# A quantized feed-forward block on one core: twelve conv spans evicted by ScalarE and GpSimd, and a reordered start

## What is computed

```python
# x (128, 32, 512); conv weight (32, 8, 9), four groups of channels
y   = conv1d(x, weight, pad=4, groups=4) + (cond @ c_weight.T + bias)[:, :, None]
gate = qlinear(y, w_gate)       # w_gate, w_up (1376, 512)
up   = qlinear(y, w_up)
out = x + qlinear(silu(gate) * up, w_down)   # w_down (512, 1376)
# qlinear(a, w): both operands rounded to whole numbers of -128..127 with a scale
# of max|row| / 127 for each row of a and each row of w, then a @ w.T
```

## Time and profile before

| what | us |
|---|---|
| median of 3 runs | 311.35 (311.17 to 311.87) |
| the profiled execution | 311.69 |
| its span in the trace | 309.9 |

### The profile page before, as it was taken

How to read it: one execution, slowest core, us unless ns; L and a number is a source line. 1 busy time by engine, 2 the same in 40 slices (tenths; PEclk the granted TensorE clock), 3 DMA queues, 4 the chain that set the end, 5 groups by cost and what they waited for, 6 DMA issues and landing times.

```text
span 309.9 us, 4607 instructions
## 1 busy us (share of the span) xinstructions
PE 286.2 (92%) x1575; PEld 168.3 (54%) x1575; DVE 257.2 (83%) x419; ACT 190.1 (61%) x217; POOL 187.2 (60%) x195
## 2 busy tenths in 40 slices
PE   0997878879799999999999999999999999999995
PEld 0987855444455555555444466566444444444543
DVE  1699669999886988897998869888988888888863
ACT  1044765797974856555688835445688866676750
POOL 1354528676745766556598855346587766666653
PEclk9999999979999999999999999999999999999999
DMA  7999503347999864443278983453366665424336
GB/s 274 419 399 401 241 1 79 76 99 160 314 364 182 192 156 114 114 109 94 75 149 228 296 218 101 104 84 101 85 151 175 164 175 124 81 80 111 86 82 215
DMA packets 80390, 51.71 MB, mean 167 GB/s; under 512 B 69520, under 2 KB 69904, under 8 KB 79472
## 3 DMA queue, kind: packets, MB, share of 16 engines
q1 hardware_dynamic: 80080, 50.80, 59.4%
q10 hardware_dynamic: 288, 0.62, 0.7%
HBM read 26.12 MB, written 8.39 MB: 111 GB/s over the span
## 4 chain that ended last, share of the span: by engine, by line
PE 63%; DVE 18%; DMA 6%; ACT 4%; issue 4%; POOL 3%; SPq 1%; DVEq 0%; POOLq 0%
PE bank L852 35%; PE bank L869 16%; PE bank L759 10%; DVE h_mem L672 4%; DMA xo_mem<-x 3%; DVE h_max L678 3%; DVE gu_max L564 3%; DMA slab<-x_blocks 2%; DVE y_part L601 2%; DVE sg_mem L662 2%; POOL sg_mem L429 2%; DVE y_mem L592 2%; DMA hq_mem<-hq_mem 1%; DVE d_max L580 1%; ACT wgu_t L476 1%
## 5 line engine op out<-in xcount | busy, mean ns | idle before, releaser
L852 PE MATMUL bank<-wgu_t,xq_mem 128*128 128x512 bf16 (+1 forms) x768 | 157.1, 360 | 9.3 <-DVE h_mem L672 6.9
L429 POOL TENSOR_TENSOR sg_mem<-sg_mem,gu_scale_row 128x512 f32<-128x512 f32 (+1 forms) x96 | 111.3, 1162 | 85.0 <-ACT sg_mem L518 84.7
L852 PEld LDWEIGHTS bank<-wgu_t,xq_mem 128*128 128x128 bf16 x768 | 74.7, 98 | 82.8 <-DVE h_mem L672 10.8
L518 ACT ACTIVATE sg_mem<-sg_mem,x_scale 128x512 f32<-128x512 f32 (+1 forms) x96 | 64.8, 676 | 65.6 <-DVE sg_mem L662 65.3
L662 DVE TENSOR_TENSOR sg_mem<-bank,gu_scale_row 128x512 f32<-128x512 f32 (+1 forms) x96 | 60.1, 627 | 23.5 <-PE bank L852 23.5
L869 PE MATMUL bank<-wd_t,hq_mem 128*128 128x512 bf16 (+1 forms) x341 | 78.2, 379 | 0.0
L672 DVE SCALAR_TENSOR_TENSOR h_mem<-bank,x_scale,sg_mem 128x512 f32<-128x512 f32 (+1 forms) x96 | 66.3, 691 | 7.7 <-POOL sg_mem L429 6.8
L523 ACT ACTIVATE h_mem<-h_mem,h_inv 128x1376 f32<-128x1376 f32 x32 | 46.1, 1441 | 21.0 <-DVE h_inv L557 21.0
L759 PE MATMUL bank<-toeplitz,slab 128*128 128x192 f32 (+1 forms) x320 | 52.7, 317 | 4.8 <-DMA slab<-x_blocks 4.8
L759 PEld LDWEIGHTS bank<-toeplitz,slab 128*128 128x128 f32 x320 | 51.3, 199 | 7.4 <-DMA toeplitz<-taps_wide 3.0
L869 PEld LDWEIGHTS bank<-wd_t,hq_mem 128*128 128x128 bf16 (+1 forms) x341 | 33.3, 98 | 40.2 <-issue 0.3
(11 more groups left out here) (54 smaller groups left out, 108.1 us busy)
## 6 DMA issues: line engine op xcount, KB each, us to landing
xo_mem<-x SPq DMA_DIRECT2D x24, 256.0 KB, 3.0
out<-xo_mem SPq DMA_DIRECT2D x24, 256.0 KB, 2.0
slab<-x_blocks SPq DMA_DIRECT2D x3, 1088.0 KB, 7.7
hq_mem<-w_gate_up SPq DMA_DIRECT2D x6, 512.0 KB, 8.7
slab<-x_blocks SPq DMA_DIRECT2D x3, 1024.0 KB, 10.2
slab<-w_down SPq DMA_DIRECT2D x3, 688.0 KB, 7.8
h_mem<-w_gate_up SPq DMA_DIRECT2D x4, 512.0 KB, 13.9
slab<-x SPq DMA_DIRECT2D x1, 2048.0 KB, 9.1
```

The costliest lines, as they stand in the source:

```text
L429: pool.tensor_tensor(s, s, gu_scale_row[:, 1, at:at + n], ALU.mult).then_inc(silu_scaled, 1)
L518: act.activation(s, s, ACT.Silu, scale=x_scale[:, i:i + 1]).then_inc(silu_done, 1)
L852: last = pe.matmul(bank[n % 2][:, 0:cols], xq_t[:, g, k, P * c:P * (c + 1)], wgu_t[:, m, k, at:at + cols], start=(k == 0), stop=(k == KT - 1))
```

## The change

Six things are changed. (1) The twelve spans 2 to 5 and 8 to 15 are no longer evicted by `add_shift`; ScalarE copies them out of PSUM (`copy_span`) and GpSimd adds the shift in place (`shift_span`); four of the twelve are in the start, eight in tiles 0 to 4 of the loop. (2) TensorE makes eight spans ahead of the loop and not twelve; spans 8 to 15 stand in tiles 0 to 4, and the folds of 9, 11, 13 and 15 in tiles 3, 3, 4 and 5. The channels of group 1 are rounded from tile 6 on, not from tile 4. (3) The first products start when eight weight tiles are turned; tiles 8, 9 and 10 and the last two rows of scales are turned between the products of tile 0, in the banks that `down` uses later. (4) TensorE runs 54 matmuls without use (`run_empty`) before x has landed. (5) The loads are in another order: weights 1, 2 and 4 come ahead of the x piece that they followed, only the taps of group 0 are loaded first, and `w_down` 0 to 2 go ahead of the second half of group 1. (6) `LEAST` is 8, so a span's last matmul has 64 columns and not 128, and the tap table is a quarter smaller. ScalarE's `round_y` moves behind the third silu of its tile.

```diff
-    LEAST = 16
+    LEAST = 2 * PAD
...
-    FRONT = 12
+    FRONT = 8
...
+        BY_ACT = [2, 3, 4, 5] + list(range(SPANS, 2 * SPANS))
+        BY_DVE = [q for q in range(SLOTS) if q not in BY_ACT]
...
+        LAST_ROWS = 5
+        W_LATE = 8
...
-        SPANS_AT = {0: [12], 1: [13], 2: [14], 3: [15]}
+        def xq_bank_of(n):
+            return xq_bank[n % 2] if n < LAST_ROWS else down_bank[n % 2]
+
+        def w_bank_of(j):
+            return w_bank[j % 2] if j < W_LATE else down_bank[j % 2]
...
+        SPANS_AT = {0: [8, 9], 1: [10], 2: [11], 3: [12, 13], 4: [14, 15]}
...
-                       for first, c, n in ((0, BY_PE, CI - BY_PE), (4, 8, CI), (13, 16, CI), (21, 24, CI))
+                       for first, c, n in ((0, BY_PE, CI - BY_PE), (6, 8, CI), (13, 16, CI), (21, 24, CI))
...
+        SHIFTS_AT = {1: [8, 9], 2: [10], 3: [11, 12], 4: [13, 14, 15]}
+        FOLDS_AT = {3: [9, 11], 4: [13], 5: [15]}
+        FOLDS_AT.update({i: [q for q in at if q % 2] for i, at in SPANS_AT.items() if at[0] >= 2 * SPANS and at[-1] % 2})
...
+        def conv_bank_free(engine, q):
+            if q in BY_ACT:
+                engine.wait_ge(conv_copied, BY_ACT.index(q) + 1)
+            else:
+                engine.wait_ge(y_ready, BY_DVE.index(q) + 1)
...
             load_w(0)
+            load_w(1)
             load_x_piece(0)
-            load_w(1)
+            load_w(2)
             load_x_piece(1)
-            load_w(2)
             load_w(3)
+            load_w(4)
             load_x_piece(2)
-            load_w(4)
             load_w(5)
             load_x_piece(3)
-            for j in range(6, JT):
+            load_w(6)
+            load_w(7)
+            sp.dma_start(toeplitz[:, 1:GROUPS, :, :].rearrange("p g c o -> p (g c o)"), taps_wide[:, CI * WIDTH:])\
+                .then_inc(taps_rest_in, 16)
+            for j in range(8, JT):
                 load_w(j)
             load_slab(1, 0)
+            for o in range(KT - 1):
+                load_w_down(o)
             load_slab(1, 1)
-            for o in range(KT):
-                load_w_down(o)
+            load_w_down(KT - 1)
...
-            for j in range(JT):
+            def shift_span(q):
+                g, i = divmod(q, SPANS)
+                span = y[g][:, :, SPAN * i:SPAN * (i + 1)]
+                pool.wait_ge(shift_ready, 1)
+                pool.wait_ge(conv_copied, BY_ACT.index(q) + 1)
+                pool.tensor_tensor(span, span, shift[:, CI * g:CI * (g + 1)].unsqueeze(2).broadcast_to([P, CI, SPAN]),
+                                   ALU.add).then_inc(y_shifted, 1)
+
+            round_w(0)
+            round_w(1)
+            shift_span(2)
+            shift_span(3)
+            round_w(2)
+            round_w(3)
+            round_w(4)
+            shift_span(4)
+            shift_span(5)
+            for j in range(5, JT):
                 round_w(j)
-
-            pool.wait_ge(w_turned, JT)
-            for b in range(HQ_BUFS):
-                pool.memset(hq[b][:, INTER:JT * P], 0.0).then_inc(pad_zero, 1)
...
+                if i == 0:
+
+                    pool.wait_ge(w_turned, JT)
+                    for b in range(HQ_BUFS):
+                        pool.memset(hq[b][:, INTER:JT * P], 0.0).then_inc(pad_zero, 1)
                 for n in CHANNELS_AT.get(i, []):
                     convert_y(n)
                 for o in down_at(i - 1):
                     convert_down(o)
                 scale_silu(i, 2)
+                for q in SHIFTS_AT.get(i, []):
+                    shift_span(q)
...
-            act.dma_start(toeplitz[:, :, :, :].rearrange("p g c o -> p (g c o)"), taps_wide).then_inc(taps_in, 16)
...
+            def copy_span(q):
+                g, i = divmod(q, SPANS)
+                act.wait_ge(conv_done, q + 1)
+                act.activation(y[g][:, :, SPAN * i:SPAN * (i + 1)],
+                               conv_bank(q)[:, :].rearrange("p (c l) -> p c l", c=CI), ACT.Copy).then_inc(conv_copied, 1)
...
-            for j in range(5):
-                copy_gate_up(j)
+            copy_span(2)
+            copy_span(3)
+            copy_gate_up(0)
+            copy_gate_up(1)
+            copy_span(4)
+            copy_span(5)
+            copy_gate_up(2)
+            copy_gate_up(3)
             copy_xq(0)
             copy_xq(1)
+            copy_gate_up(4)
             copy_gate_up(5)
-            copy_gate_up(6)
+            copy_xq(2)
+            copy_xq(3)
             round_y(0)
             round_y(1)
+            copy_gate_up(6)
+            copy_xq(4)
             copy_gate_up(7)
-            copy_xq(2)
-            copy_xq(3)
-            copy_xq(4)
-            copy_gate_up(8)
-            copy_gate_up(9)
-            copy_xq(5)
-            copy_gate_up(10)
-            copy_xq(6)
...
+            silu(0, 0)
+            copy_gate_up(8)
+            silu(0, 1)
+            copy_gate_up(9)
+            copy_gate_up(10)
+            copy_xq(5)
+            copy_xq(6)
             for i in range(TILES):
-                silu(i, 0)
-                silu(i, 1)
+                if i:
+                    silu(i, 0)
+                    silu(i, 1)
                 if i == DOWN_ROW_AT + 1:
                     copy_down_row()
                 for o in down_at(i - 1):
                     round_down(o)
-                for n in CHANNELS_AT.get(i, []):
-                    round_y(n)
                 if i:
                     round_h(i - 1)
                 silu(i, 2)
+                for n in CHANNELS_AT.get(i, []):
+                    round_y(n)
+                for q in SPANS_AT.get(i, []):
+                    if q in BY_ACT:
+                        copy_span(q)
                 if i:
...
-                dve.wait_ge(y_ready, q + 1)
+                if q in BY_ACT:
+                    dve.wait_ge(y_shifted, BY_ACT.index(q) + 1)
+                else:
+                    dve.wait_ge(y_ready, BY_DVE.index(q) + 1)
...
@@ -619,38 +690,38 @@
                               ALU.add).then_inc(shift_ready, 1)
             weights_top(1)
             weights_scale(0, 2)
+            weights_inverse(0, 2)
+            weights_top(2)
             dve.wait_ge(shift_ready, 1)
             add_shift(0)
-            weights_inverse(0, 2)
-            for q in range(1, 7, 2):
-                weights_top(q + 1)
-                add_shift(q)
-                weights_top(q + 2)
-                weights_scale(q + 1, 2)
-                fold_y(q)
-                weights_inverse(q + 1, 2)
-                add_shift(q + 1)
+            add_shift(1)
+            weights_top(3)
+            weights_scale(2, 2)
+            fold_y(1)
+            weights_inverse(2, 2)
+            weights_top(4)
+            weights_top(5)
+            weights_scale(4, 2)
+            fold_y(3)
+            weights_inverse(4, 2)
+            weights_top(6)
+            add_shift(6)
+            weights_top(7)
             add_shift(7)
+            weights_scale(6, 2)
+            fold_y(5)
+            weights_inverse(6, 2)
+            fold_y(7)
+            group_top(0)
+            group_scale(0)
+            group_inverse(0)
             weights_top(8)
-            fold_y(7)
             weights_top(9)
-            group_top(0)
             weights_scale(8, 2)
-            group_scale(0)
             weights_inverse(8, 2)
-            group_inverse(0)
             weights_top(10)
-            add_shift(8)
             weights_scale(10, 1)
-            add_shift(9)
             weights_inverse(10, 1)
-            add_shift(10)
-            fold_y(9)
-            add_shift(11)
-            fold_y(11)
-            for o in down_at(-1):
...
+                else:
+                    for o in down_at(-1):
+                        weights_down(o)
                 multiply_up(i, 0)
+                if i == 0:
+                    multiply_up(i, 1)
                 if i >= LAG:
                     scale_down(i - LAG)
                 scale_gate(i, 2)
                 for q in SPANS_AT.get(i, []):
-                    add_shift(q)
-                multiply_up(i, 1)
-                for q in SPANS_AT.get(i, []):
-                    if q % 2:
-                        fold_y(q)
+                    if q in BY_DVE:
+                        add_shift(q)
+                if i:
+                    multiply_up(i, 1)
+                for q in FOLDS_AT.get(i, []):
+                    fold_y(q)
                     if q % SPANS == SPANS - 1:
                         group_top(q // SPANS)
...
+                if q == SPANS:
+                    pe.wait_ge(taps_rest_in, 16)
                 if q >= 4:
 
-                    pe.wait_ge(y_ready, conv_before(q) + 1)
+                    conv_bank_free(pe, conv_before(q))
...
-                if j >= 2:
+                if W_LATE <= j < W_LATE + 2:
+
+                    conv_bank_free(pe, FRONT - 2 + j - W_LATE)
+                elif j >= 2:
...
-                if n >= 2:
```

(83 more changed lines are left out.)

13 lines of the change are left out of this document (7 added, 6 removed).

## The result

The changed kernel takes 320.36 us, median of 4 runs (319.0 to 322.23), against 311.46 (311.17 to 311.87) before: 1.026 times as long, interval 1.022 to 1.030. The forecast was 310.2, with a range of 307.6 to 313.0. The profiled execution took 322.23, its span 320.5, 10.6 more than before.

What follows compares the result with a forecast made beforehand. It took TensorE alone as the bound from about 100 to 281 us, with the start and tiles 0 to 4 ahead. Span 309.9 - 0.4 - 0.75 = 308.75, plus 1.79 outside, less 0.34 for the median: 310.2, range 307.6 to 313.0.

Steps and rivals of the forecast that it cites:

- later rounding leaves one tile to the DMA turn: Group 1's channels, rounded later: one tile (8.4) is left to the DMA turn, listed as costing nothing.
- The walk: Queues followed through tiles 0 to 3: h_max at 47.2, 56.6, 66.45 and 75.65, the last 76.38 before.
- all given back: Tiles 0 to 4: GpSimd's and ScalarE's queues return the early start's gain; the loop's start gains 0.4, not 11.
- The rival that the queues hold up less: Tiles 1 to 3: half of VectorE's 6.3 us idle is absent, everything behind 3.1 earlier, 307.1; chance 0.14.
- First product: Start: the first product begins at 30.2 instead of 41.48, with x_inv at 26.8 instead of 31.49.
- the lifted rate: Start: empty matmuls ahead of x bring spans 0 and 1 to full rate, worth 2.7 us.
- The third gate piece: Tile 0: runs from 39.9 to 40.7; eleven microseconds at the first product are five here.
- The rival of the half clock: Gaps of 2.3 and 3.1 in tiles 1 and 2 halve TensorE's clock, two spells cost 2.6: 312.8; chance 0.18.
- The narrow matmul: TensorE-bound stage, spans 18 to 31: 64 columns less, 0.054 for each of 14 spans, 0.75; ends 0 and 1.5.
- The last gap: TensorE's gap of 0.73 before 99.21, from the late residual, shrinks by 0.25 to 0.73; 0.4 taken.
- Covered for nothing: List of effects expected to cost nothing: GpSimd's memsets, later taps, w_down loads, later rounding of group 1, the tail.
- The eviction by ScalarE: Moved span evictions: 0.59 on ScalarE and 1.28 on GpSimd instead of VectorE's 0.68.

Runs made afterwards that it cites:

- changed kernel with fill: Changed kernel plus 42 empty matmuls on TensorE in four waits of the start, ScalarE's order as changed: 318.75 us, 1.021 of before.
- its second run: The changed kernel itself, measured again beside the kernel before at 312.67, nothing altered: 319.62 us, 1.024 of before.
- the kernel with the fill: Changed kernel with round_y ahead of round_h and the third silu again, plus 42 empty matmuls in four waits of the start: 302.95 us, 0.970 of before.
- the first experiment: Changed kernel with one thing undone, round_y ahead of round_h and the third silu again in every tile: 303.32 us, 0.972 of before.

## Why the prediction was wrong

**The step that failed** is the place of `round_y`. The prediction named the move, walked it in tiles 0 to 2, and then wrote that later rounding leaves one tile to the DMA turn and that TensorE alone bounds the rest. The move holds in every tile that rounds channels, and there are twelve beside the first three. In tiles 6 to 9 a tile also has a span, 8.4 us of TensorE, and the 8.43 us of the new chain are just hidden. In tiles 13 to 16 and 21 to 24 TensorE has 7.03, and each round of the chain is 1.4 longer. That is the 9.8 us behind tile 12; it shows at seven gaps and not eight, because the chain of tile 16 ends in tile 17, whose two spans hide it. It is shown from both sides: with the order back, the stretch from tile 12 to the end takes 157.8 and not 167.6; with the move alone in the kernel before, 167.6 and not 157.8. The prediction had put it at nothing, without a reason. A stage is bound by one engine only as long as every other chain through a tile is shorter than that engine's work; I had checked the sums of busy time and not that chain.

**The loss in tiles 0 to 4.** The walk put `h_max` at 47.2, 56.6, 66.45 and 75.65. With the full clock in the start (changed kernel with fill) they are 47.13, 56.44, 65.75 and 74.99. TensorE's span of tile 6 begins at 92.09 there and at 93.12 before: 1.0 ahead, where the forecast of "all given back" had nothing. Folds 11 and 13 wait for GpSimd's shift, 1.17 and 2.22 us in the changed kernel, as walked (2.7 for fold 13). So the walk was nearly right in its times. But its reason was wrong. I put it down to the load on GpSimd and ScalarE, 8.5 and 7.35 us a tile. With the order back and the same load, tile 3 is at 68.88, 6.8 ahead of the walk. The walk held the order and I read load out of it. That the times agree is in part luck: the walk had no half clock in it, and the kernel with fill had it from 58 to 65, where sixteen matmuls took 6.09 and not 3.36. The rival that the queues hold up less, 307.1, was nearer to what the rest of the change is worth. (It halves 6.3 us of idle time "in tiles 1 to 3"; the four figures that make up the 6.3 are those of tiles 0 to 3.)

**The start.** First product 29.90 to 30.93 in the kernels that start as the changed one does, against 30.2 forecast: right, and with it the 4.7 us of VectorE work taken from ahead of `x_inv` and 2.0 of the 2.7 for the lifted rate. The third gate piece, forecast for 39.9, begins in the changed kernel at 42.8, since the first product was 0.7 late and its twelve matmuls took 4.91 and not 2.76:

```profile
30.00:32.00 2.00, 1.07 (x3) 0.44 (x4) 1.46 (x3) 1.79 (x2) 2.00 (x4) 0.50 1.06 442
```

The columns are those of the earlier trace rows; the granted clock is 0.50. I had weighed half clock for the gaps in tiles 1 and 2 only, and it comes in the start too, and again behind the gap before 52.8. The profile of the changed kernel is 2.7 behind the one with the fill at tile 12 (152.90 against 150.18), but 1.0 of that stands ahead of the first product (30.93 against 29.94). Of it 0.6 is x, which landed late: the first spans begin at 8.29, in its second run at 7.68. In the medians the fill is worth 0.9. The rival of the half clock was thus real, but the smaller part.

**The narrow matmul.** Forecast 0.75 for the stage, 1.37 for a span; measured 1.37, but 0.6 from tile 0 to tile 31, and about 0.5 of it in the stage. The sum counted 14 spans at 0.054. Spans 24 to 31 come in pairs, and a pair saves 0.05 once, so it should have counted ten. The Trainium skill (TensorE: Matmul & The Clock Gate, LDWEIGHTS) gives P / 1.2 ns for loading P columns, 107 ns for 128. By that the narrow matmul gains nothing wherever a further such load follows, and the trace agrees: a pair of spans gains 0.05 (2.79 against 2.84) and not twice that. Where a bf16 product follows, the 0.05 agrees with one of the two narrow instructions still covering such a load and the other giving back its half. That last is argued from the size and not shown by itself.

**The last gap.** The residual's wait is gone in the changed kernel: GpSimd's residual add (L479) waits for no DMA, only three times for VectorE's `hq_mem`, where the earlier trace rows has the late landing. With the fill it waits 0.9 for that DMA again, and TensorE has no gap there all the same. TensorE's gap of 0.73 is gone in the changed kernel and in those made from it, as the prediction had it at best. "Covered for nothing" missed by little: at 106.98 of the changed kernel's profile TensorE waits 0.28 for the DMA turn of a channel that is now rounded later.

**The moved instructions.** The eviction by ScalarE takes 0.57 to 0.60 (0.59 forecast). GpSimd's shift takes 1.04, less than the 1.28 of the row that I took for it.

What stays open: how the 4 us of the early start part into clock and start, since no run made that change with the clock held; and what makes up the last 1.0 us between the sum of the parts undone here (2.0 + 0.6 + 1.5 + 4 = 8.1) and the 9.1 that the kernel with the fill gains. The gap of 0.73 that is gone would fit half of it: from the span of tile 5 to that of tile 7 the first experiment takes 17.19 us and the kernel before 17.79, of which 0.1 is the narrow matmul. It was not tried by itself. No run undid the reordered loads or VectorE's new order in the start.

## What to carry to other kernels

When one engine's queue is reordered, look at every place where the loop does it, not at the stage the change is about, and follow it to the engines that wait: an instruction moved behind another is a new wait for whatever stands behind its consumer. Before you call a stage bound by one engine, follow the chain of waits through one round until it comes back to the instruction where it began, and add it up. What it is shorter than that engine's time is the slack, here 0.3 us (6.74 against 7.03), and a move can use it up. If two engines hand each other two streams, give both the same order; here either order did, 303.32 and 304.11.

## What the runs showed of the hardware

TensorE's clock fell to half behind waits that are short by themselves, and their length does not tell when. Ahead of the first twelve product matmuls stand three waits between turns. With 1.52, 0.72 and 1.11 us the twelve took 4.91 (changed kernel), with 0.59, 0.72 and 1.13 they took 4.43 (its second run), and with 0.60, 0.71 and 1.13 they took 2.89 (`round_y` back) and 4.45 (with the wide matmul). With 1.51, 0.71 and 1.12 they took 2.89 (without the empties ahead of x) and 5.30 (the order undone from tile 6 on). The granted clock of the executions of one kernel differs too, 1.0 and 0.994 with `round_y` back. With the 30 empty matmuls in these three places the longest idle time there was 0.35, and the twelve took 2.89 in both kernels profiled so. The executions of the faster one lie within 0.8 us; those of the five kernels without this fill that have the two queues in matching order lie 0.4, 1.7, 2.1, 3.2 and 4.0 apart, so one of them was steady without it, and the fill is not shown to be needed for that. The full clock in the start did not keep it later: behind 2.11, 0.84 and 2.36 us it fell again.

Two prices: a float32 addition of 128x512 on GpSimd takes 1.04 us where its second input is one value per channel spread over the span (`shift_span`), and 1.27 where both inputs are full (the residual add). A float32 span whose last matmul has 64 columns and not 128 is 0.05 us shorter when a bf16 product follows it, and not measurably when another span does (2.79 for two against 1.37 for one; 2.84 and 1.42 with the wide one).
